# GroupNorm and attention over 1024 rows: straight code, scores of two rows in succession, three places for P

## What is computed

```
g = v.reshape(B_, H_, W_, 32, C_ // 32)
m = mean(g, axis=(1, 2, 4)); s = var(g, axis=(1, 2, 4))
n = ((g - m) / sqrt(s + eps)).reshape(v.shape)
qkv = einsum('bglc,dc->bgld', n, W_qkv) + b_qkv
score = softmax(einsum('bghlc,bghmc->bghlm', q, k) / C ** 0.5)
out = x + einsum('bghlm,bghmc->bghlc', score, v)
```

## Time and profile before

| | |
|---|---|
| median of 3 runs | 3886.53 us (3881.05 to 3887.36) |
| the profiled execution | 3887.38 us, span 3885.6 us |
| PE busy | 3790.3 us (98%) |
| DVE busy | 3713.4 us (96%) |
| ACT busy | 3081.1 us (79%) |
| POOL busy | 2429.5 us (63%) |
| granted TensorE clock | 0.997 of full |

### The profile page before, as it was taken

The page is one execution under the profiler, slowest core; times in us unless marked ns, Lnnn a source line. Parts: engine busy times, 40 slices in busy tenths (PEclk is TensorE's granted clock), DMA queues, the critical chain, the costliest instruction groups (busy, mean ns, idle before and its releaser), DMA issues.

```text
span 3885.6 us, 144060 instructions
## 1 busy us (share of the span) xinstructions
PE 3790.3 (98%) x44133; PEld 2976.9 (77%) x44133; DVE 3713.4 (96%) x6114; ACT 3081.1 (79%) x8193; POOL 2429.5 (63%) x3089
## 2 busy tenths in 40 slices
PE   4999999999999999999999999999999999999998
PEld 3777777777777777777777777777777777777777
DVE  5999999999999999999999999999999999999998
ACT  2788878888788887878878788787888888888786
POOL 1657566575665656566575665756657566575787
PEclk9999999999999999999999999999999999999999
DMA  7999999999999999999999999999999999998988
GB/s 188 215 210 216 214 210 214 213 213 214 210 214 209 214 216 209 213 210 214 215 209 215 211 215 211 211 213 209 212 210 212 215 213 213 211 205 182 177 179 177
DMA packets 2441865, 809.15 MB, mean 208 GB/s; under 512 B 2179072, under 2 KB 2441600, under 8 KB 2441600
## 3 DMA queue, kind: packets, MB, share of 16 engines
q1 hardware_dynamic: 2311040, 679.97, 89.7%
q10 hardware_dynamic: 130560, 125.86, 11.8%
HBM read 134.42 MB, written 134.22 MB: 69 GB/s over the span
## 4 chain that ended last, share of the span: by engine, by line
PE 50%; DVE 29%; issue 12%; ACT 4%; POOL 2%; DVEq 2%; DMA 1%; SPq 0%; ACTq 0%; POOLq 0%
PE s_pair L298 14%; PE qk_bank L276 14%; PE o_bank L314 10%; DVE p_lo L437 10%; DVE neg_max L429 10%; PE v_bank L286 6%; DVE bn L461 4%; ACT prob L394 3%; PE xt_bank L268 3%; POOL p_hi L600 2%; PE v_bank L283 1%; DVE o_norm L456 1%; DVE rsum L449 1%; DVEq L461 1%; DVE v_lo L443 1%
## 5 line engine op out<-in xcount | busy, mean ns | idle before, releaser
L600 POOL TENSOR_SCALAR p_hi<-prob 128x1024 f16<-128x1024 f32 x1024 | 1072.7, 1048 | 1403.1 <-ACT prob L394 1105.4
L394 ACT ACTIVATE prob<-s_pair,neg_max 128x256 f32<-128x256 f32 x4096 | 1610.8, 482 | 256.2 <-DVE neg_max L429 115.3
L437 DVE SCALAR_TENSOR_TENSOR p_lo<-prob,p_hi 128x1024 f16<-128x1024 f32 x1024 | 1357.7, 1326 | 54.8 <-POOL p_hi L600 37.2
L429 DVE TENSOR_REDUCE neg_max<-s_pair 128x4 f32<-128x1024 f32 x1024 | 1238.6, 1210 | 16.0 <-PE s_pair L298 15.1
L374 ACT ACTIVATE qk<-qk_bank,b_in 128x256 f32<-128x256 f32 x2048 | 861.5, 472 | 482.0 <-PE qk_bank L276 476.1
L298 PE MATMUL s_pair<-qk 64*128 64x256 f32 x8192 | 1164.7, 403 | 1.2 <-ACT qk L374 1.0
L276 PE MATMUL qk_bank<-xc,w_norm 128*128 128x256 f32 x4096 | 1160.1, 406 | 0.0
L616 POOL TENSOR_TENSOR y_ring<-image,o_norm 128x256 f32<-128x256 f32 x1024 | 1042.5, 1018 | 4.4 <-DMA out_dram<-y_ring 3.0
L276 PEld LDWEIGHTS qk_bank<-xc,w_norm 128*128 128x128 f32 x4096 | 695.1, 189 | 393.1 <-issue 337.7
L314 PE MATMUL o_bank<-v_hi,pt_lo 128*128 128x65 f16 x8192 | 851.2, 193 | 37.4 <-issue 19.5
L298 PEld LDWEIGHTS s_pair<-qk 64*128 64x128 f32 x8192 | 707.1, 186 | 219.8 <-issue 171.9
(11 more groups left out here) (72 smaller groups left out, 2075.9 us busy)
## 6 DMA issues: line engine op xcount, KB each, us to landing
out_dram<-y_ring SPq DMA_DIRECT2D x512, 256.0 KB, 2.8
image<-in_x_dram ACTq DMA_DIRECT2D x480, 256.0 KB, 3.4
pt_hi<-p_hi SPq DMA_TRANSPOSE x1024, 3.8
pt_lo<-p_lo SPq DMA_TRANSPOSE x1024, 3.2
image<-in_x_dram SPq DMA_DIRECT2D x4, 2048.0 KB, 16.3
w_in<-in_L_conv_W_qkv_dram SPq DMA_DIRECT2D x1, 192.0 KB, 2.4
b_in<-in_L_conv_b_qkv_dram SPq DMA_DIRECT2D x3, 0.5 KB, 2.1
```

The costliest lines, as they stand in the source:

```text
L394: ins = act.activation(prob[:, m, c:c + TOK], s_bank[m][h][:, a * TOK:(a + 1) * TOK], ACT.Exp, bias=neg_max[:, m, h, a:a + 1])
L429: dve.tensor_reduce(neg_max[:, m, :, :].rearrange("p h a -> p (h a)"), s_pair[m][:, :].rearrange("p (b k) -> p b k", b=HEADS * J), AX.X, A ...
L437: dve.scalar_tensor_tensor(out=p_lo[:, v % 2, :], in0=prob[:, v % 2, :], scalar=P_SCALE, in1=p_hi[:, v % 2, :], op0=ALU.mult, op1=ALU.subt ...
L600: pool.tensor_scalar(p_hi[:, v % 2, :], prob[:, v % 2, :], P_SCALE, 1.0, ALU.mult, ALU.mult).then_inc(phi_done, 1)
```

## The change

There are no loops: the schedule is one straight list of 1040 steps per engine. On every even block PE makes the scores of that block and of the next, one after the other; the projections of q and k and the transpose run one block further ahead. Each other engine has an order for even and one for odd steps. P high and P low have three places each instead of two, with a semaphore each. x_ring and its copies go: PE transposes from the image. The 32 moments are spread over rows 8 to 47 (40 rows), the 23 steps over rows 48 to 63, and the load of the image after next begins 8 rows behind instead of 20, so that 28 instead of 22 loads of two rows are issued in the first eight steps. Cut to its core:

```diff
-    FINISH = 12
-    STATS_FROM = ROWS - FINISH - GROUPS
+    FINISH = 16
+    STATS_FROM = 8
-    X_AHEAD = 2
+    X_AHEAD = 3
...
-        p_hi = sb("p_hi", [P, 2, QK], F16)
-        p_lo = sb("p_lo", [P, 2, QK], F16)
+        p_hi = sb("p_hi", [P, 3, QK], F16)
+        p_lo = sb("p_lo", [P, 3, QK], F16)
...
-        STAT_MM_AT = (0, 2, 6)
+        STAT_MM_AT = (0, 4, 11)
+        STAT_OPS_AT = {0: ((1,),), 1: ((2,), (3,)), 2: ((4,), (5,)), 3: ((6,), (7,)), 5: ((8, 9), (10,)),
+                       6: ((11,), (12,)), 7: ((13,), (14,)), 8: ((15,), (16,)), 9: ((17,), (18,)),
+                       10: ((19,), (20,), (21,)), 12: ((22,), (23,))}
...
+                if 0 <= img < IMAGES - 1 and 0 <= row - STATS_FROM < MEASURE_ROWS:
+                    group = (row - STATS_FROM) * GROUPS // MEASURE_ROWS
+                    if group != (row - STATS_FROM - 1) * GROUPS // MEASURE_ROWS:
+                        what = (MEASURE, img + 1, group)
...
+                order(run, next_image, i % 2)
+            for i in range(-2 * UNROLL, BLOCKS + 2 * UNROLL):
+                step(i)
...
         # SP
-                run(-2, transpose_low)
-                run(-7, store)
-                run(-1, transpose_high)
+                run(-1, transpose_low)
+                run(-6, store)
+                run(0, transpose_high)
         # PE
-                run(0, scores)
-                run(+1, project_qk)
+                if not odd:
+                    run(0, scores)
+                    run(+1, scores)
+                run(+2, project_qk)
                 run(0, project_v)
                 next_image(0)
                 run(-3, values)
-                run(+3, x_transpose)
+                run(+4, x_transpose)
         # ACT
                 next_image(0)
-                run(-1, exponent, 0)
-                run(-1, exponent, 1)
-                run(+2, x_copy)
-                run(+1, qk_copy)
+                if not odd:
+                    run(+3, x_copy)
+                run(0, exponent, 0)
+                run(0, exponent, 1)
+                if odd:
+                    run(+3, x_copy)
+                run(+2, qk_copy)
                 run(0, v_high)
         # DVE
-                run(-2, p_low)
+                if odd:
+                    run(0, row_max)
                 run(-4, sums)
                 next_image(0)
                 run(-1, v_low)
                 next_image(1)
                 run(-4, divide)
                 next_image(2)
-                run(0, row_max)
+                if not odd:
+                    run(0, row_max)
+                run(-1, p_low)
                 next_image(3)
                 next_image(MEASURE)
         # POOL
                 run(0, p_high)
-                run(+6, refill)
                 run(-4, finish)
```

More of the change, by code:

```diff
@@ L177, in next_image @@
                 def next_image(place):
                     if what is not None and (place == MEASURE) == (what[0] == MEASURE):
[L179 to L216, removed]
@@ L218, in schedule @@
-            run_image(0, 0, True, False)
-            for img in range(1, IMAGES):
-                run_image(img, img % 2, False, img == IMAGES - 1)
+                        share(0, i, par, what, place)
+                if bring is not None:
+                    if 0 <= i < 2 * UNROLL:
+                        for c in range(i, CHUNKS - LAG // LOAD_ROWS, 2 * UNROLL):
+                            bring(i, 1, 1, c * LOAD_ROWS)
+                    if coming is not None and row % LOAD_ROWS == 0:
+                        bring(i, *coming)
@@ L267, in x_transpose @@
                 for j in range(J):
-                    mm = pe.transpose(xt_bank[:, j * P:(j + 1) * P], x_ring[:, m, j * C:(j + 1) * C], ident[:, :])
+                    mm = pe.transpose(xt_bank[:, j * P:(j + 1) * P], image[:, par, row, j * C:(j + 1) * C], ident[:, :])
                 mm.then_inc(xt_done, 1)
@@ L347, in share, with order @@
                     statistics(what[1] * STAT_STEPS, STAT_MM_AT.index(what[2]))
-            def order(run, next_image):
-                run(0, scores)
-                run(+1, project_qk)
+            def order(run, next_image, odd):
+                if not odd:
+                    run(0, scores)
+                    run(+1, scores)
+                run(+2, project_qk)
                 run(0, project_v)
@@ L403, in share, with order, bring @@
                     act.wait_ge(stat_step, (what[1] + 1) * STAT_STEPS)
-            def order(run, next_image):
+            def order(run, next_image, odd):
                 next_image(0)
-                run(-1, exponent, 0)
-                run(-1, exponent, 1)
-                run(+2, x_copy)
-                run(+1, qk_copy)
+                if not odd:
[5 more added lines that the diff above has]
+                run(+2, qk_copy)
                 run(0, v_high)
-            def bring(base, u, img, par, row, free=False):
-                if not (free or base is None or known_below(base, LAG)):
-                    act.wait_ge(y_done, base + (u + LOAD_ROWS - LAG))
+            def bring(i, img, par, row):
+                if i >= LAG:
+                    act.wait_ge(y_done, i + LOAD_ROWS - LAG)
                 rows = bass.ds(row, LOAD_ROWS)
@@ L434, in p_low @@
                 dve.wait_ge(phi_done, base + (v + 1))
[L435 to L438 removed]
+                if not known_below(base, 3 - v):
+                    dve.wait_ge(lo_in[v % 3], landed(base, v - 3))
+                dve.scalar_tensor_tensor(out=p_lo[:, v % 3, :], in0=prob[:, v % 2, :], scalar=P_SCALE,
+                                         in1=p_hi[:, v % 3, :], op0=ALU.mult,
                                          op1=ALU.subtract).then_inc(plo_done, 1)
@@ L628, in _, with order @@
             pool.memset(half_ones[:, :], 2.0 / P).then_inc(const_done, 1)
-            pool.wait_ge(first_in[0], 16)
-            def order(run, next_image):
+            def order(run, next_image, odd):
                 run(0, p_high)
-                run(+6, refill)
                 run(-4, finish)
```

67 lines of the change are left out of this document (28 added, 39 removed).

## The result

The changed kernel took 4049.01 us, the median of 4 runs (4042.49 to 4050.37), against 3886.82 (3881.05 to 3887.36) for the kernel before in the same comparison. The ratio is 1.0415, 95% interval 1.0400 to 1.0429: slower by 4.2%. The forecast was 3982 us, slower by 2.5%.

What follows compares the result with a forecast made beforehand. PE bounded the kernel at 3.66 us per row, DVE filling the same time where moments are taken. Fifteen images +90, last image +0.7, start +4: 3887.4 + 94.7 gives 3982 us, range 3905 to 4080.

Steps and rivals of the forecast that it cites:

- a ring of three engines: Waits among ACT, DVE and PE from one odd row's x_copy to the next, forecast longer than PE's pair: 7.34 us.
- PE's 0.50 us: On PE, one entry into and one exit from the scores saved per pair of rows: at most 0.17 + 0.33 us.
- rival 1: PE's saving is the whole story: pairs without moments 6.82 us, with moments 7.30, in all 3726 us; chance 0.05.
- the pair with a moment: Pair with a moment in the even row, where row_max(e+1) gates exp(e+1): 7.77 us, 16 pairs an image.
- Rival 2: On DVE, bn of the even row does not delay exp(e+1): all pairs 7.34 us, about 3878 us; chance 0.08.
- the pair without a moment: Pair without a moment in its even row: 2.23 + 5.11 = 7.34 us, against 7.32 before.
- PE waits for x_copy(e+4) before it may transpose row e+5: With e the even row, ACT's copy gates PE's transpose and the next scores behind it, putting PE's saving inside the loop.
- I take 0.25: 2.2 us per image: Six of 23 statistics steps on the loop between v_low and row_max: w_norm 0.92, others 0.25 each; bounds 0.9 and 2.7.
- the other steps stand where DVE waits: On DVE, statistics steps other than the six on the loop stand where it waits for v_high or ACT.
- Rival 3: y_ring may hold p_low(e-1), now on the loop; margin 0.2 to 1.5 us; 4260 us if always lost; chance 0.12.
- Rival 4: Straight code has more instructions to fetch, 210 more packets: up to +280 us; chance that it shows 0.06, then around 4100.
- The start: First image, with 28 instead of 22 loads in the first eight steps: +4 us, bounds 16 less and 16 more.

Runs made afterwards that it cites:

- the kernel with the old orders: The changed kernel with the orders of PE, ACT, DVE and SP put back as in the kernel before, scores of one row per step: 3861.23 us, ratio 0.9941.
- the last run: Changed kernel with late moment, split exponent, y_ring behind P low, and statistics steps except o_bank readers in even rows beside P low: 3850.85 us, ratio 0.9908.

## Why the prediction was right, and where it was not

**Right: that a ring of three engines replaces PE as the bound,** so that PE's 0.50 us are not seen. PE's busy share fell to 92%, and the pair rose instead of falling, so rival 1 is out. The kernel with the old orders shows that the rest of the change does not slow it.

**Right: the pair with a moment,** 7.77 forecast, 7.82 measured, for the reason given and by the ring given. Keeping the moment back took the pair to 7.45 and 83 us off the time. Rival 2 would have had the exponent reach its place later than the maximum; ACT waited 0.29 us instead.

**Mis-sized: the pair without a moment,** 7.34 forecast, 7.45 measured. The step that failed is "PE waits for x_copy(e+4) before it may transpose row e+5". In blocks 450 to 452 that x_copy ended at 1817.66 and PE came to the transpose 0.27 us later. PE waits earlier in its queue, for q/k copy before the q/k product of row e+3, and everything behind it follows in PE's order. I followed DVE's and ACT's queues to the end and PE's only from one point. The forecast ring itself was 0.08 short, mainly since V high lasts 0.49 there. Together with the shortfall of 0.05 in the moment pairs this is 1.5 us an image, 21 us in 14 images.

**Wrong: "I take 0.25: 2.2 us per image" for the statistics,** and that "the other steps stand where DVE waits". The eight pairs cost 4.2 us over eight of 7.45, beyond the upper bound of 2.7. From start to start, without idle time, the 23 steps take DVE 9.9 us an image in the changed kernel, 5.9 before and 3.2 with the old orders. They filled DVE's list to 8.3 us, so DVE was no longer waiting where they stood. The earlier trace rows showed 347 ns for one step whose kind lasts 171 when undisturbed; I read it as the step's cost, and it already was half waiting. So was w_norm's 0.92: in the last run it lasts 0.415. This is 40 us of the 60 that the forecast lacked, by 2.8 us in 14 images.

**Rival 3 named the right mechanism at the wrong place.** P low and y_ring do not meet in the changed kernel (1220 and 726 ns on average), as the margin of 0.2 to 1.5 us said: in blocks 450 to 452 y_ring ends 1.17 us before that P low begins. (The rows behind the least margin, 0.13 + 1.05 + 1.70, give 2.88 and not 3.2.) But the statistics meet P high and y_ring, which I did not look at, and P low met y_ring as soon as an experiment shortened the ring. The Trainium skill (SBUF — State Buffer, Who interferes with whom) says that a GpSimd instruction that reads SBUF contends for a shared port pair with a DVE instruction that has two SBUF inputs, and with a tensor_scalar or a copy in a two-port mode; whichever starts first keeps the pair for its whole instruction. The traces agree: a tensor_scalar with one input lasted 0.90 beside P high and 0.18 beside nothing. That it ran in such a mode no row here shows.

**Rival 4 fell:** with 361 instruction packets the kernel with the old orders is faster than before. **The start** was put at 4 us more and took 4 us less: the first image takes 12.2 us more than the others, before 16.2. No run bears on it.

**Luck: that the time lies inside the range.** The bounds of the terms reached 4010 us. What took the range up to 4080 was room for rivals 3 and 4, and neither came about in the form described.

What stays open: which of the two rings, 0.03 us apart, would bound a pair without moments if the other were cut alone. No run cuts one alone; that PE's comes last is read from the timeline.

## What to carry to other kernels

When an order of several in-order engines is rewritten, add up every ring, and follow each engine's queue through the ring from the first instruction that waits: the bound need not be on the engine that was relieved. Take the cost of a small DVE instruction from a row where POOL runs nothing beside it, and place it by what POOL does at that moment; where it stands can matter five times more than what it does. An instruction that is lengthened by such sharing shows as busy, so compare its length with the shortest of its kind before calling an engine full.

## What the runs showed of the hardware

- Steps on 128x32 elements last 0.15 to 0.19 us alone (group means of the kernel with the old orders and of the last run) and as much as 1.02 beside POOL: one that began 0.06 us behind the start of P high (1.04 us) ended 0.04 us behind its end.
- The delay goes both ways: P high lasted 1.74 us instead of 1.04 when P low was running at its start.
- Such a delay need not cost time: in the kernel with the old orders, where PE sets the pace, rows 48 to 63 take 59.3 us with the copy into wide at 0.21 us and at 1.07.
- Not all DVE work is held: the maximum, which reads s_pair in PSUM, lasted 1.22 us with P high beginning inside it (2255.33 and 2255.45 in the run with the steps where POOL is idle), and P high kept its 1.04.
- Two dependent steps in a row cost little by themselves: 2253.57 to 2253.77, 0.20 us, against 0.10 from the second step to an instruction that does not depend on it.
